# Masking the diagonal blocks of the maxima: on VectorE instead of by products on TensorE

## The reference

```python
y = einsum('bse,ef->bsf', x, W1) + b1          # q, k, v for 16 heads
w = einsum('bhqd,bhkd->bhqk', q, k) / dk
mask = tril(ones((S, S)))
w = w * mask - NEG_BIG * (1.0 - mask)          # causal: a query sees keys up to itself
w = softmax(w, axis=-1)
attn = einsum('bhqk,bhkd->bhqd', w, v)
x = x + (einsum('bse,ef->bsf', attn, W2) + b2)
```

## Time and profile before

| | |
|---|---|
| timed executions, median | 3347.27 us |
| the profiled execution's own time | 3338.09 us |
| its span, from first to last instruction | 3336.3 us |
| mean granted clock of TensorE | 0.91 of full speed |
| the dense attention's groups | about 1714 to 3076 us of the span |
| a group, from S0 to the next S0 | 41.5 to 50.1 us |

### The profile page before, as it was taken

One profiled execution on the slowest core, in us unless ns is written; L12 is line 12 of the kernel. 1 busy time (PEld: TensorE's weight loads), 2 busy tenths in 40 slices (PEclk: granted clock), 3 DMA queues, 4 the chain that ended last, 5 costly groups with the idle time before them and its releaser, 6 DMA issues. The chain is left out here.

```text
span 3336.3 us, 100799 instructions
## 1 busy us (share of the span) xinstructions
PE 2725.8 (82%) x45778; PEld 1532.3 (46%) x45778; DVE 1638.9 (49%) x2761; ACT 1434.9 (43%) x1419; POOL 795.8 (24%) x545
## 2 busy tenths in 40 slices
PE   2688887879787787688669999898999898998787
PEld 1455555646465555433334444444444444443433
DVE  3345443434444444520666666666666666664601
ACT  0444544444445443230135455555545455555511
POOL 3333434333424341000312222222212121211001
PEclk9788898888888887799679999999999999999998
DMA  6333434343434332469032222222222222220398
GB/s 181 91 99 84 103 82 104 74 103 82 115 81 110 83 92 63 127 283 413 11 86 58 58 58 59 58 58 50 55 42 57 58 58 49 58 58 2 150 421 337
DMA packets 265295, 351.59 MB, mean 105 GB/s; under 512 B 146650, under 2 KB 173956, under 8 KB 248484
## 3 DMA queue, kind: packets, MB, share of 16 engines
q1 hardware_dynamic: 235316, 314.16, 33.0%
q10 hardware_dynamic: 29552, 30.97, 3.8%
HBM read 273.97 MB, written 68.71 MB: 103 GB/s over the span
## 5 line engine op out<-in xcount | busy, mean ns | idle before, releaser
L1387 DVE TENSOR_REDUCE b_tops<-b_slot 128x8 f32<-128x1024 f32 x576 | 680.4, 1220 | 354.7 <-PE b_slot L1242 179.1
L1428 ACT ACTIVATE b_probs<-b_slot 128x1024 f32<-128x1024 f32 x576 | 582.4, 1022 | 546.0 <-PE b_slot L1242 393.5
L525 POOL COPY a_q_far<-a_q_near 96x1024 bf16<-96x1024 bf16 x128 | 258.6, 2050 | 342.7 <-PE a_slot L616 203.7
L1189 POOL TENSOR_SCALAR_AFFINE_SELECT b_probs<-b_probs 128x1024 f32<-128x1024 f32 x128 | 139.6, 1091 | 801.4 <-ACT b_probs L1428 801.4
L1262 PE MATMUL b_outT_ps<-b_probs,b_v 128*17 128x128 f32 (+3 forms) x4608 | 317.9, 383 | 6.1 <-ACT b_probs L1428 5.5
L1242 PE MATMUL b_slot<-b_q_stack,b_k_stack 99*128 99x512 bf16 (+3 forms) x1280 | 272.9, 320 | 44.0 <-DVE b_tops L1387 32.8
L913 ACT ACTIVATE a_k_far<-a_k_near 96x1024 bf16<-96x1024 bf16 x128 | 258.2, 2067 | 115.7 <-DMA a_k_near<-parts_near_dram 106.9
L1242 PE MATMUL b_slot<-b_k_stack,b_q_stack 96*128 96x512 bf16 (+3 forms) x1280 | 265.8, 322 | 29.4 <-DVE b_tops L1387 20.6
L813 DVE TENSOR_TENSOR a_probs<-a_slot,a_bias_k 128x1024 f32<-128x1024 f32 x128 | 154.7, 1219 | 190.8 <-PE a_slot L616 190.7
L822 DVE TENSOR_REDUCE a_tops<-a_slot 128x16 f32<-128x1024 f32 x128 | 156.3, 1222 | 131.4 <-PE a_slot L616 130.3
L876 ACT ACTIVATE a_probs<-a_probs 128x1024 f32<-128x1024 f32 x128 | 133.2, 1052 | 174.6 <-DVE a_probs L813 150.8
(11 more groups left out here) (228 smaller groups left out, 4241.4 us busy)
## 6 DMA issues: line engine op xcount, KB each, us to landing
f_w_ring<-in_L_ffn_w_dram SPq DMA_DIRECT2D x128, 1024.0 KB, 15.6
parts_near_dram<-a_parts ACTq DMA_DIRECT2D x96, 256.0 KB
parts_dram<-b_parts SPq DMA_DIRECT2D x96, 256.0 KB
a_k_near<-parts_near_dram SPq DMA_DIRECT2D x128, 128.0 KB, 2.9
b_k_stack<-parts_dram SPq DMA_DIRECT2D x64, 256.0 KB, 6.9
a_q_near<-parts_near_dram SPq DMA_DIRECT2D x64, 192.0 KB, 3.0
b_q_stack<-parts_dram SPq DMA_DIRECT2D x32, 384.0 KB, 4.5
values_dram<-a_v_stage SPq DMA_DIRECT2D x16, 544.0 KB, 4.2
```

What stands on the lines that cost most here:

```text
L525: pool.tensor_copy(q_far[far][0:QK_ROWS, h, :].rearrange("p (r a) -> p r a", r=LINKS), q_near[near][0:QK_ROWS, h, :].rearrange("p (a r) -> ...
L1189: pool.affine_select(out=blocks, in_=blocks, compare_op=ALU.is_ge, fill=0.0, base=0, pattern=[[0, NT], [1, P]], channel_multiplier=-1).the ...
L1387: ins = dve.tensor_reduce(out, src, AX.X, ALU.max)
L1428: act.activation(probs_of(b, g, u, h)[:, :], slot_of(step)[:, :], ACT.Exp).then_inc(taken_act, 1)
```

## The change

The two identity products of each diagonal mx unit are left out, and its 8 products start their PSUM regions themselves. VectorE takes such a unit in two instructions in place of one. The first adds later (broadcast over the 8 blocks) to the PSUM tile and writes the sum to the SBUF tile full; the slot counts as taken when it ends. The second takes the maxima from full. The second waits for the first, and the next diagonal unit's add waits for the second, through a new semaphore mx_diagonal. Since full is also the tile of the q and k steps, an add waits for every part2 that stands ahead of it in seq, and a q or k step waits for the diagonal units ahead of it. mred waits for the group's diagonal maxima too.

```diff
+        elif step[0] == "part2":
+            n_parts += 1
+        elif step[0] == "mx":
+            parts_before[step] = n_parts
+            n_diagonals += step[3] == 0
+        elif step[0] in ("q", "k"):
+            diagonals_before[step] = n_diagonals
...
                         if u == 0:
-                            for c in range(2 if kind == "mx" else 0):
-                                pe.matmul(dst[:, 512 * c:512 * (c + 1)], ident16[:, :], later[:, :].unsqueeze(1).to_broadcast([P, 4, P]),
-                                          start=True, stop=False, skip_group_check=True)
                             for tile in range(NT):
                                 mine = slice(P * tile, P * tile + P)
-                                ins = pe.matmul(dst[:, mine], own[0:rows, h, mine], other[0:rows, h, mine], start=kind == "S", stop=True,
+                                ins = pe.matmul(dst[:, mine], own[0:rows, h, mine], other[0:rows, h, mine], start=True, stop=True,
                                                 skip_group_check=True)
...
                         dve.wait_ge(taken_dve, count("taken_dve", "mx", b, g, UNITS - 1, HG // 2 - 1))
+                        dve.wait_ge(mx_diagonal, HG * (b * G + g + 1))
...
+                            if u == 0:
+                                hold(dve, part2_done, parts_before[step])
+                                hold(dve, mx_diagonal, HG * (b * G + g) + h)
+                                masked_scores = full[:, :].rearrange("p (c k) -> p c k", k=P)
+                                dve.tensor_tensor(masked_scores, src, later[:, :].unsqueeze(1).to_broadcast([P, NT, P]), ALU.add).then_inc(taken_dve, 1)
+                                dve.wait_ge(taken_dve, nth["taken_dve", step])
+                                dve.tensor_reduce(out, masked_scores, AX.X, ALU.max).then_inc(mx_diagonal, 1)
+                                continue
                             ins = dve.tensor_reduce(out, src, AX.X, ALU.max)
...
                             hold(dve, part2_done, count("qk", *step) - 1)
+                            hold(dve, mx_diagonal, diagonals_before[step])
                             ins = dve.tensor_scalar(full[:, :], src[:, :], bqk[:, m, half:half + 1], None, ALU.add)
```

More of the change, by code:

```diff
@@ L1084, in last_unit @@
         return "S", b, g, UNITS - 1, HG // 2 - 1
-    last_pieces = {}
+    last_pieces, parts_before, diagonals_before, n_parts, n_diagonals = {}, {}, {}, 0, 0
     for step in seq:
@@ L1126, in dense_attention @@
             sem(n) for n in ("masked", "pv_done", "ote_done", "z_ready", "mred_chain", "mred_done", "recip_done"))
-        part0_done, rest1_done, part1_done, part2_done, mrows_in = (
-            sem(n) for n in ("part0_done", "rest1_done", "part1_done", "part2_done", "mrows_in"))
+        part0_done, rest1_done, part1_done, part2_done, mrows_in, mx_diagonal = (
+            sem(n) for n in ("part0_done", "rest1_done", "part1_done", "part2_done", "mrows_in", "mx_diagonal"))
         spilled = [sem(f"spilled{n}") for n in range(2)]
```

## The result

The changed kernel takes 3539.36 us (three executions, 3527.15 to 3542.0), against 3347.27 before: a ratio of 1.056, with a 95% interval of 1.052 to 1.059. It is slower by 192 us; 3527 us was forecast.

The account below looks back on a forecast made before the run. The prediction took VectorE to bound a group's start and PE the later part. It added 118 us for VectorE's queue and 62 us for PE's slow clock, 180 in all, to 3347: 3527 us, range 3450 to 3572.

Parts of the forecast that it names:

- The bound: In a group's first 11 us VectorE sets the end; behind S4 PE is the bound, at 90% busy.
- The queue: Group start: a diagonal unit takes 2.50 us of VectorE instead of 1.14, so S4 starts 3.7 us later; 118 us together.
- The first group's 3.8 us: First group, 18 maxima end to end on VectorE: added time less what m0's earlier fill gives, 3.8 us.
- What was saved: Identity products removed from PE: 0.44 us a diagonal unit, 56 us in all, counting only before m0 in the group start.
- The clock: PE's clock falls in each of 31 groups' starts, costing 2.0 us behind S4; 62 us, ends 40 and 87.
- the walk: PE's units from S4 on at slow clock: full clock 3.1, 4.8 or 6.5 us later costs 1.3, 2.0 or 2.8 us.
- The waits on full: Adds wait for earlier part2, q and k steps for earlier diagonals; both at nothing, with 2.4 us clear for the add.
- Two readings that were off: Readings of the kernel before: VectorE's waits before m0 4.2 to 4.5 us, groups 41.5 to 50.1 us long.
- PE as the bound: Rival: PE bounds throughout and VectorE's added work goes into its idle time; 3291 to 3347 us, chance 3%.
- A clock that does not fall: Rival: PE's clock does not fall in the group starts, or its fall costs nothing; 3466 us, chance 20%.
- A fast maximum from SBUF: Rival: VectorE's diagonal maximum from SBUF takes 0.753 us, 60 us less; 3467 us with the fall, 3406 without; chance 4%.
- an add held by GpSimd: Rival: GpSimd's masks hold VectorE's add up to 1.1 us each, or the clock falls longer; 3527 to 3660 us, chance 5%.

Follow-up runs that it names:

- e1_queue: Kernel before, identity products kept, plus one more VectorE maximum with unused result, from a constant SBUF tile, behind each diagonal maximum; 3518.0 us, ratio 1.050.
- e4_spread: Changed kernel with the four diagonal mx units at places 0, 2, 5 and 8 of a group's 18 instead of 0 to 3; 3422.5 us, ratio 1.022.
- e7_wide: Changed kernel with diagonal mx units at places 0, 4, 8 and 12 and masked scores in tile zb instead of full; 3438.3 us, ratio 1.027.
- e3_warm: Changed kernel plus 15 unused identity products a group on PE, in units S2, m3, m4, S3 and m5; 3479.6 us, ratio 1.038.
- e2_no_mask: Kernel before without the identity products and with no mask in the diagonal maxima; 3315.4 us, ratio 0.990.

## Why the prediction was right

**The bound.** It held that in a group's first 11 us VectorE sets the end, though the shares point to PE. e1_queue and e4_spread confirm it, the one by adding VectorE's time, the other by only moving it. Behind S4 it held that PE is the bound. e7_wide, which moves most of the added VectorE time there, bears this out in the main: where its clock stays full, the 5.4 us of VectorE time that the prediction counts for a group lengthen it by 1.0 us, and not by the 4.0 of e3_warm's groups (45.6 us at full clock).

**The queue.** 3.68 us up to S4 were forecast and 4.04 measured. The durations were right to 5 ns. The term that was mis-sized is the pause ahead of a waiting instruction: 0.03 us was taken for all, which holds from add to maximum; from a maximum to the next add it is 0.13, three times a group. That is 0.3 of the 0.36 us. The first group's 3.8 us came out as 4.1. Together 118 us were forecast, and e3_warm's stretch gives 124 for the 31 groups, and 4 for the first.

**What was saved.** The prediction counted only m0's 0.44 us of the four pairs' 1.76 against the new queue, and that fits: the first add starts 1.11 us behind S0, where m0's maximum started at 1.54. In the kernel before, the removal alone brings S4 forward by 1.09 us, since the 0.94 us wait before m2 shortens too, and gives 27 us in all and not 55. In the changed kernel the queue covers that wait, and the gain of the other pairs is idle time of PE.

**The clock.** It was forecast to fall in each group and to cost 2.0 us, 62 in all; 2.04 and 64 us were measured, and the trace has the fall in all 31 groups. The slow clock is 10.1 us a group in the mean. Of these 4.5 lie ahead of S4, where they cost nothing, and 5.6 behind it. The falls end 3.1 to 6.3 us behind S4, which is the range, 3.1 to 6.5, for which the walk was made. That the middle value of the walk came out to within 2 us in all is partly luck: nothing singled it out, and six of the groups with g = 0 have a second fall of 3.4 us, 44 us behind S0, which the walk does not have. The Trainium skill's advice in "TensorE: Matmul & The Clock Gate", in the section on why this matters for kernels, which lays a fall to one long idle gap, is not borne out here either: the longest gap before the fall in the timeline above is 1.5 us.

**The waits on full** cost nothing of their own, as forecast, beside the 0.03 us each.

**Two readings that were off.** The waits before m0 are 3.1 to 4.9 us long in the 30 groups, and not 4.2 to 4.5, and the groups before are 33.3 to 51.0 us long, and not 41.5 to 50.1: the last two have less work. In the changed kernel they are 38.5 to 56.2. Neither enters the sum.

**The rivals.** PE as the bound: out by e1_queue and e2_no_mask. A clock that does not fall: e3_warm has it, at 3480 us against the 3466 worked out for it, but only with filler products. A fast maximum from SBUF and an add held by GpSimd: out by 1220 and 1225 ns. The Trainium skill's smaller fixed part for SBUF in "VectorE: DVE Perf Modes", in the section on the TRN2 errata, does not show: the maximum takes 1220 ns from SBUF and 1219 from PSUM.

## What to carry to other kernels

Read the bound in the stretch where a change puts its work, not from a share over the phase: VectorE was 63% busy, and had no room where these 128 instructions went. Weigh what moves in the queue's own unit: 0.44 us of PE work was traded for a 1.22 us VectorE instruction. And where a new wait thins out TensorE's work for some us, price the slow clock behind it too; here it was a third of the loss, and products that nothing uses took it away. When a trace has groups of the same work with and without a fall of the clock, compare those first: their difference is the clock's price. In e4_spread and e7_wide it is what tells a fall of the clock from a queue on VectorE.

## What was not expected of the hardware

Filler products cost nothing while the engine would wait, and they kept the clock up: 15 products a group, 0.99 instead of 0.90 over the groups, 60 us less. The clock fell in all 31 groups though no idle gap of PE from S0 to S4 is longer than 1.64 us. Here PE is 2.53 us busy in the 6.04 ahead of the fall (the changed kernel):

```profile
2273.60:2279.64 6.04, 2.53 (x35) 1.83 (x32) 5.57 (x6) 2.79 (x3) 2.19 (x2) 1.00 0.71 123
```

One fall of 3.4 us costs between 0.8 and 1.6 us, by the groups of equal work with and without one.

An instruction that waits for its forerunner on VectorE starts 0.03 us after it in one pair (add, then maximum) and 0.10 to 0.13 in the other (maximum, then add); why is open.
